# Expert layer of a graph kernel on one core: second-layer products two groups behind the first-layer products, with three ReLU buffers

## The reference

```python
logits = xf @ router_w.T + router_b
idx = jnp.argmax(logits, axis=-1)
h = jax.nn.relu(jnp.einsum('nd,ndh->nh', xf, jnp.take(W1, idx, axis=0)) + jnp.take(b1, idx, axis=0))
out = jax.nn.relu(jnp.einsum('nh,nhd->nd', h, jnp.take(W2, idx, axis=0)) + jnp.take(b2, idx, axis=0))
```

## Time and profile before

| what | us |
|---|---|
| timed runs | 789.2, 786.34, 785.68 |
| median | 786.34 |
| profiled execution, its own time | 789.66 |
| its span on the core | 787.8 |
| granted TensorE clock, mean over the span | 0.885 |
| PE busy / DVE / ACT / POOL in the span | 597.6 / 386.8 / 163.6 / 455.2 |

### The profile page before, as it was taken

How to read it: one execution, slowest core, us unless ns; L and a number is a source line. 1 busy time by engine, 2 the same in 40 slices (tenths; PEclk the granted TensorE clock), 3 DMA queues, 4 the chain that set the end, 5 groups by cost and what they waited for, 6 DMA issues and landing times.

```text
span 787.8 us, 10439 instructions
## 1 busy us (share of the span) xinstructions
PE 597.6 (76%) x3180; PEld 478.0 (61%) x3181; DVE 386.8 (49%) x1272; ACT 163.6 (21%) x345; POOL 455.2 (58%) x464
## 2 busy tenths in 40 slices
PE   0467787798987877799888977997879894388960
PEld 0356676575766656577666766776657762276850
DVE  3844444332332344445746656466555766822552
ACT  0450000000000001013323322223123252144420
POOL 9146666666666666666756666666666600452263
PEclk9969998889899996799989989798989996588985
DMA  8462333323333344334333443333433417452021
GB/s 227 157 185 83 92 89 94 95 83 96 87 87 94 87 116 138 84 92 132 117 106 108 128 134 101 114 108 106 134 98 112 128 49 216 131 170 61 28 89 51
DMA packets 41872, 86.78 MB, mean 110 GB/s; under 512 B 11280, under 2 KB 23378, under 8 KB 41491
## 3 DMA queue, kind: packets, MB, share of 16 engines
q0 software_dynamic: 22576, 61.01, 26.9%
q1 hardware_dynamic: 18372, 22.95, 9.4%
q10 hardware_dynamic: 864, 2.08, 1.2%
HBM read 73.21 MB, written 12.80 MB: 109 GB/s over the span
## 4 chain that ended last, share of the span: by engine, by line
PE 56%; issue 12%; DVE 8%; DMA 7%; POOL 6%; another core or an unknown queue 6%; ACT 2%; SPq 1%; DVEq 0%; POOLq 0%; ACTq 0%
PE ps L789 24%; PE ps L831 10%; PE ps L820 6%; POOL gath L535 5%; DMA gath<-xn_d,src_i 4%; PE ps L1028 3%; PE ps L796 2%; PE ps L1037 2%; DMA both<-in_x 2%; PE ps L803 2%; PE ps L853 2%; PE ps L843 1%; POOL both L562 1%; PE ps L808 1%
## 5 line engine op out<-in xcount | busy, mean ns | idle before, releaser
L535 POOL DMA_INDIRECT gath<-xn_d,src_i x392 | 383.5, 978 | 224.8 <-issue 88.2
L789 PE MATMUL ps<-wmat,gath 128*128 128x144 f32 x1568 | 263.8, 312 | 31.0 <-DMA gath<-xn_d,src_i 10.9
L789 PEld LDWEIGHTS ps<-wmat,gath 128*128 128x128 f32 x1568 | 233.2, 205 | 59.9 <-issue 21.9
L1192 DVE TENSOR_TENSOR acc_raw<-acc_raw,ps 128x144 f32 x392 | 101.9, 301 | 277.8 <-PE ps L789 189.5
L1165 DVE TENSOR_TENSOR wmat<-hit,wts 128x576 f32<-128x576 f32 x100 | 75.3, 753 | 0.2
L562 POOL DMA_INDIRECT both<-rows_d,inv_i x25 | 24.3, 972 | 59.4 <-DVE inv_i L1439 47.0
L831 PE MATMUL ps<-wq_wv,acc_raw 128*128 128x256 f32 (+1 forms) x200 | 53.0, 390 | 0.0
L831 PE MATMUL ps<-wk_et,acc_raw 128*128 128x256 f32 (+1 forms) x200 | 53.0, 390 | 0.0
L1485 DVE SCALAR_TENSOR_TENSOR acc_raw<-ps,wts,acc_raw 128x256 f32 x56 | 27.0, 482 | 51.7 <-PE ps L1037 34.0
L820 PE MATMUL ps<-cmat,both 128*128 128x512 f32 (+1 forms) x100 | 51.5, 640 | 0.0
L567 POOL DMA_INDIRECT out<-acc_raw,inv_i x25 | 25.3, 1014 | 40.8 <-DVE acc_raw L1476 34.4
(11 more groups left out here) (194 smaller groups left out, 623.0 us busy)
## 6 DMA issues: line engine op xcount, KB each, us to landing
gath<-xn_d,src_i POOLq DMA_INDIRECT x392
rows_d<-both SPq DMA_DIRECT2D x24, 256.0 KB
both<-in_x SPq DMA_DIRECT2D x24, 128.0 KB
both<-in_x SPq DMA_DIRECT2D x4, 640.0 KB, 16.8
xn_d<-both SPq DMA_DIRECT2D x4, 640.0 KB
acc_raw<-in_w_t SPq DMA_DIRECT2D x1, 2080.0 KB
acc_raw<-in_w_t SPq DMA_DIRECT2D x1, 2048.0 KB, 7.5
acc_raw<-in_type_rows ACTq DMA_DIRECT2D x1, 1600.0 KB, 15.1
```

What stands on the lines that cost most here:

```text
L535: g.indirect_dma_start(gath[:, k, :], None, xn_d, bass.IndirectOffsetOnAxis(ap=src_i[:, OCT * q + k:OCT * q + k + 1], axis=0)).then_inc(ga ...
L789: ins = t_.matmul(ps_edge[quarter][:, m * B * WIN:(m + 1) * B * WIN], gath[:, k, m * P:(m + 1) * P], wmat[:, k, :, :].rearrange("p b w -> ...
L1192: d.tensor_tensor(place, place, ps_edge[w][:, m * B * WIN:(m + 1) * B * WIN].rearrange("p (b w) -> p b w", w=WIN), ALU.add).then_inc(added, 1)
```

## The change

TensorE's order becomes `hidden(g)`, `turn_tiles(g + 1)`, `outer(g - 2)`, and after the loop `outer(12)` and `outer(13)`. The ReLUs get a third buffer, a view of `wmat`, which is free in this stage; ACT's wait for a free buffer moves by one group with it. The expert numbers of two groups are kept in registers. DVE writes ones into the bias row of the third buffer with one more memset. The wait for the second-layer weights moves to the first `outer`.

```diff
-        f_hts = gath_flat[0:H + 1, 2 * FT * KD * H:2 * FT * (KD * H + P)].rearrange("p (j s n) -> p j s n", j=2, n=P)
+        f_hts2 = gath_flat[0:H + 1, 2 * FT * KD * H:2 * FT * (KD * H + P)].rearrange("p (j s n) -> p j s n", j=2, n=P)
+        f_hts = [f_hts2[:, 0, :, :], f_hts2[:, 1, :, :], wm_flat[0:H + 1, 0:FT * P].rearrange("p (s n) -> p s n", n=P)]
...
-                if g >= 2:
-                    act.wait_ge(f_out, FT * (g - 1))
+                if g >= 3:
+                    act.wait_ge(f_out, FT * (g - 2))
...
-                    s.activation(f_hts[0:H, g % 2, f, :], ps[4 + g % 2][0:H, f * P:(f + 1) * P], ACT.Relu,
+                    s.activation(f_hts[g % 3][0:H, f, :], ps[4 + g % 2][0:H, f * P:(f + 1) * P], ACT.Relu,
...
-                        t_.matmul(ps[g % 2 * 2 + f // 2][:, f % 2 * D:(f % 2 + 1) * D], f_hts[:, g % 2, f, :],
+                        t_.matmul(ps[g % 2 * 2 + f // 2][:, f % 2 * D:(f % 2 + 1) * D], f_hts[g % 3][:, f, :],
...
-                experts = None
+                experts = {}
...
-                    if g == 1:
+                    if g == 2:
                         pe.wait_ge(w2_loaded, 16)
-                    if g > 0:
-                        outer(g - 1, experts)
-                    experts = row_values(pe, pair_i[0:1, 0, FT * g:FT * (g + 1)], X - 1, CLAMPED)
-                outer(NG - 1, experts)
+                    if g > 1:
+                        outer(g - 2, experts[g % 2])
+                    experts[g % 2] = row_values(pe, pair_i[0:1, 0, FT * g:FT * (g + 1)], X - 1, CLAMPED)
+                outer(NG - 2, experts[NG % 2])
+                outer(NG - 1, experts[(NG - 1) % 2])
...
-                at = o.mark(d.memset(f_hts[H:H + 1, :, :, :], 1.0))
+                o.mark(d.memset(f_hts2[H:H + 1, :, :, :], 1.0))
+                at = o.mark(d.memset(f_hts[2][H:H + 1, :, :], 1.0))
```

## The result

| | before | changed |
|---|---|---|
| median of 8 runs | 787.59 | 790.3 |
| lowest and highest run | 784.36, 789.68 | 786.85, 794.82 |
| ratio to before, with its 95% interval | | 1.0053 (1.0027 to 1.0079) |
| profiled execution: its time, its span, mean clock | 789.66, 787.8, 0.885 | 791.32, 789.6, 0.881 |

The changed kernel is slower, by a ratio that is some 4.2 us; the medians are 2.7 us apart. Two later comparisons of the same pair gave 1.0031 (0.9998 to 1.0064) and 1.0035 (1.0011 to 1.0059). Weighted by their intervals, the three make 1.0041 (±0.0016), that is 3.2 us, 2.0 to 4.4. I had forecast +0.8 us and "the same". The time lay in the range, the sum was too small.

The account below looks back on a forecast made before the run. The end was taken as first store, plus 25 stores at POOL's rate, plus pauses from late TensorE results. Terms 0 + 0 + 0 + 3.8 + 0 - 3.0 = +0.8 us gave a median of 787.1 from 786.34, range 783.0 to 791.3.

Parts of the forecast that it names:

- Second memset: Before the first groups: 0.46 us more memset, hidden under ACT's wait for a gathered tile; cost 0, at most +0.5.
- o0 leaves the front: Between the transposes and h2: h2's completion is seen late anyway, so 0, bounds -1.8 to +1.7.
- step 4: At POOL's first store, which waits for o7: it starts one round of TensorE's own stretch later, +3.8 us.
- upper bound of +1.7: At h2, after o0 leaves: the completion delay only lengthens, or TensorE drops to half clock for one h.
- Rounds 3 to 13: Middle rounds: same h, transposes and loads, with one o of the same size and a smaller number; 0.
- First pause unchanged: After nine stores: the same 4.1 us pause, so store 10 starts at 760.9; 0.
- step 6: Last stores: POOL never lacks rows, the 3.36 us second pause goes; -3.0 us, bounds -3.4 to +1.8.
- A: At the tail: late completions hold all twelve last products, +4.9, so 791.2 us; chance 0.14.
- D: At the tail: the second pause stays as long, only the later start counts, +3.8, 790.2 us; chance 0.12.
- B: After nine stores: the 4.1 us pause belongs to a place in time and goes, 782.0 us; chance 0.14.
- C: Near 700 us, o0's old place: a further half-clock stretch costs about 3.3 us, 790.4 us; chance 0.08.

Follow-up runs that it names:

- experiment 4: Changed kernel with second-layer products three groups behind and four ReLU buffers: 790.67 us against 784.77 for before, ratio 1.0071.
- experiment 2: Changed kernel, but products two groups behind only in rounds 2 to 5, then one behind: 785.15 us against 784.77 for before, ratio 1.0004.
- experiment 8: o4 ahead of round 5's transposes, last gather 128 rows, against before: two behind from round 8, 0.9954 (first edit alone 0.9999); old order, 0.9970.
- experiment 7: All 25 stores held until every row is finished, against before at 777.29 us: kernel before 796.67, ratio 1.0249; changed kernel 799.74, ratio 1.0288.
- experiment 5: Changed kernel unaltered, measured twice more against before: 779.34 us against 777.29, ratio 1.0031; 787.65 against 786.03, ratio 1.0035.

## Why the prediction was right, and where it was not

1. *Second memset, 0.* It held. It took 0.48 us, and h0 started 9.2 us behind the first gather (688.28) where it was 9.3; the buffers alone gave 0.9991. The row of ACT's copy names "issue" ahead of it (0.60 us idle now, 1.23 before), so the wait for a tile that I had read there is not shown.
2. *o0 leaves the front, 0.* It held: the ReLUs of h2 began behind a late completion as before (705.59, idle 3.15 us against 3.25). o0's 1.99 us had to be done later, where TensorE is the bound; in my sum they stand in step 4, whose round of 3.8 us is one h and one o. I did not see that this is where they come from. The upper bound of +1.7 had other reasons, and adding it would count o0 twice.
3. *Rounds 3 to 13, 0.* The rounds keep their length.
4. *First store one round later, +3.8.* It measured +4.1 and +4.0 against the two profiles of before at the same clock (67.1; 63.0 and 63.2), and +3.4 for the next round (experiment 4). Of it 1.6 is o0's (experiment 2) and 2.2 the tail's, one more h ahead of o7 (experiment 8). These make the 3.8; the 0.2 to 0.3 beyond it no run names.
5. *First pause unchanged.* 4.19 against 4.08; 3.73 and 4.15 in the two further profiles.
6. *Second pause gone, -3.0.* This is the step that failed, in its size and in part of its reason. The pause is gone in all three profiles of the change, and against the two profiles of before that is worth 3.0 to 3.3 us from the first store to the last (35.1 to 35.3; 38.3 and 38.5). But the same order with three buffers needed only 37.4 (pause 2.60, clock 0.86), 2.1 to 2.3 more than the change, and the pair of experiment 8 differs by 2.3 (pause 2.85, clock 1.00). I took one execution's pause for the kernel's. As for the reason: I said that o11 and most of o12 and o13 would be computed before completions become late again, near 765. They took until 771, 9 us into the run of stores, and the late completions never set in; had they come where I placed them, 6 us ahead of TensorE's last product, part of the pause might have stayed. Why they stayed away no run shows. That the pause went entirely was in part luck.

By the profiles with equal clocks the change therefore costs 0.8 to 1.1 us, which is what I had summed, and with the smaller gains of step 6 it would be about 1.7 to 2.0 (4.0 to 4.1, less 2.1 to 2.3; this is a sum, not a run). The comparisons say 3.2, 2.0 to 4.4. So the sign of the sum fits, and the profiles account for a quarter to somewhat over half of the measured size. Where the rest arises stays open: executions already differ by up to 15 us in the 670 us ahead of this stage (first gathers from 667.0 to 681.7), and by 4 us through the clock near the last tile, so single profiles can't settle a difference of 1 us. How often each kernel has that half-clock stretch would need many profiles; it wasn't tried, and it is the rival that is left. The few profiles there are point the other way: the stretch is in both of before and in one of three of the change.

Of the rivals, A (a second pause with all twelve last products late) and D (the second pause stays) didn't appear in any of the three profiles. B fell by experiment 7; the stretch near 700 us that C asked for is in one of the three and cost nothing there (experiment 5). That the late completions follow POOL's run of indirect DMAs was only read off three places in the prediction; experiment 7 shows for the stores that there are none without them. For the gathers it wasn't tried. The reading of the Trainium skill (Perfetto Trace Analysis, the lifecycle of a TensorE instruction), that a matmul's shown end is an estimate and no completion, agrees with the trace: 6.5 us lay between the row's end and the release with stores running, and 0.14 us with stores held. Whether the passes ran late or were only reported late these rows do not show.

The chances were too sure of "the same": with a forecast of +0.8 and a gain of 3.0 that rested on one pause of one execution, there was more room above +0.8 than below it, and "slower" deserved more than 0.23. That 790.3 lies within the range says little: the range was wide enough to hold both a gain and a loss.

## What to carry to other kernels

If what a group of consumers releases is a queue that works at a fixed rate to the end, delaying the group delays the end: find what starts that queue, and price the change there first. Work taken out of rounds where it was covered must be priced where it lands, not where it left. A pause can be regained only once, so two edits that each pay for themselves out of it needn't pay together; and its size has to be read from more than one execution.

## What the runs showed of the hardware

- While POOL issued output DMAs back to back, TensorE's results could reach the other engines late: 6.5 us for one h, and a drain of 10.9 us. With the stores held the drain took 0.07 us. In all twelve profiles with free stores POOL ran out of rows after nine stores, for 2.8 to 4.2 us. The delay is not there in every run of stores: in the second run of the changed kernel nothing was late in any of three profiles, and the drain took 0.43, 0.07 and 0.07 us. How this comes about no run here shows.
- Behind holes of 0.46 to 1.16 us inside h13, TensorE's granted clock fell to its lower level: 0.50 in the changed kernel's last window. The Trainium skill (TensorE: Matmul & The Clock Gate, part 1) ties the clock to how busy the array was, and that agrees. But the same program went through the 12 us around the wait for the last tile at 0.72 in one execution and at 1.00 in two others, which was worth 3.5 to 4.0 us at the first store.
- An indirect gather of 53 rows held POOL for 1.57 us, where one of 128 rows takes 0.95. Asking for 75 rows more made the slowest landing fall from 8.1 to 3.9 us; it was 7.7 to 8.1 us in all twelve profiles with 53 rows, and 3.9 and 4.0 in the two with 128.
